# Layer 0 of a graph network: six ranges of destinations instead of four in the dense product, and the last two squares turned in another PSUM bank

## What is computed

```python
def _L0_gnn_ref(x, edge_row, edge_col, edge_val, W):
    msgs = edge_val[:, None] * x[edge_col]
    agg = jax.ops.segment_sum(msgs, edge_row, num_segments=N_NODES)
    return agg @ W.T
...
edge_index = jnp.stack([src, dst])
x = _layernorm(x + _L0_gnn_ref(x, src, dst, edge_weight, L0_gnn_W), axis=-1)
```

## Time and profile before

| | |
|---|---|
| median of 3 runs | 3743.57 us (3740.58 to 3748.71) |
| the profiled execution's own time | 3747.34 us |
| its span, first to last instruction | 3745.8 us |
| busy shares of the span | PE 79%, POOL 66%, DVE 53%, ACT 32% |
| scatters of the loop (L1744) | 572, from 37.0 to 1186.4 us |

### The profile page before, as it was taken

The page is one execution under the profiler, slowest core; times in us unless marked ns, Lnnn a source line. Parts: engine busy times, 40 slices in busy tenths (PEclk is TensorE's granted clock), DMA queues, the critical chain, the costliest instruction groups (busy, mean ns, idle before and its releaser), DMA issues. The chain is left out here.

```text
span 3745.8 us, 60018 instructions
## 1 busy us (share of the span) xinstructions
PE 2964.1 (79%) x19220; PEld 2154.1 (58%) x19220; DVE 2002.0 (53%) x6486; ACT 1185.7 (32%) x3717; POOL 2469.5 (66%) x2238
## 2 busy tenths in 40 slices
PE   5999888899985958887488885778887664888885
PEld 4776666577764834444366643556666653455553
DVE  8899888888973933323223353233434542243447
ACT  5565656677874920001000043001111321011113
POOL 3888888887876756663656666666666554666653
PEclk9999999999997979998688865888889876999997
DMA  7788788899987954553344456444554437566664
GB/s 261 109 137 134 134 134 137 146 164 165 164 153 148 359 151 125 136 137 91 91 115 117 123 158 208 122 133 144 157 152 143 141 115 232 160 174 172 175 169 128
DMA packets 544385, 572.47 MB, mean 153 GB/s; under 512 B 84446, under 2 KB 492428, under 8 KB 542540
## 3 DMA queue, kind: packets, MB, share of 16 engines
q0 software_dynamic: 153600, 258.41, 35.6%
q1 hardware_dynamic: 316622, 251.54, 22.0%
q10 hardware_dynamic: 73854, 58.70, 5.0%
HBM read 376.38 MB, written 192.04 MB: 152 GB/s over the span
## 5 line engine op out<-in xcount | busy, mean ns | idle before, releaser
L908 POOL DMA_INDIRECT rows_buf<-T,idx x888 | 849.0, 956 | 491.9 <-issue 237.9
L1744 POOL DMA_INDIRECT A<-rows_buf,big x572 | 913.6, 1597 | 252.1 <-issue 147.9
L1002 PE MATMUL PSA<-S,rows_buf 128*128 128x128 bf16 (+2 forms) x5904 | 624.4, 260 | 289.5 <-issue 182.7
L1058 DVE TENSOR_TENSOR accT<-PSA,accT 128x256 f32 (+2 forms) x354 | 132.5, 374 | 1214.8 <-remote 772.4
L1002 PEld LDWEIGHTS PSA<-S,rows_buf 128*128 128x128 bf16 (+2 forms) x5904 | 553.7, 148 | 382.5 <-issue 239.0
L908 POOL DMA_INDIRECT rows_buf<-X,idx x528 | 505.3, 957 | 273.2 <-issue 143.0
L1414 PE MATMUL PSA<-XRS,rows_buf 128*128 128x256 f32 x1144 | 311.0, 396 | 0.6 <-ACT rows_buf L1426 0.6
L1577 DVE TENSOR_TENSOR accT<-PSA,accT 128x392 f32 (+5 forms) x366 | 238.0, 650 | 73.5 <-PE PSA L1523 26.9
L818 ACT ACTIVATE accT<-accT,vec 128x500 f32<-128x500 f32 (+3 forms) x26 | 17.6, 693 | 798.7 <-DVE accT L816 403.9
L1426 ACT ACTIVATE rows_buf<-PSA 128x512 f32<-128x512 f32 x286 | 168.6, 594 | 206.2 <-PE PSA L1414 169.6
L940 PE MATMUL PSA<-XRS,accT 128*128 128x512 fp8e4 x686 | 219.4, 400 | 10.6 <-issue 10.2
(11 more groups left out here) (322 smaller groups left out, 5779.1 us busy)
## 6 DMA issues: line engine op xcount, KB each, us to landing
XRS<-Ad SPq DMA_DIRECT2D x200, 256.0 KB
XRS<-in_xpad SPq DMA_DIRECT2D x192, 128.0 KB
Ad<-accT SPq DMA_DIRECT2D x224, 98.0 KB
A<-accT SPq DMA_DIRECT2D x12, 1568.0 KB
Awd<-accT SPq DMA_DIRECT2D x48, 392.0 KB
rows_buf<-T,idx POOLq DMA_INDIRECT x888
rows_buf<-A SPq DMA_DIRECT2D x24, 512.0 KB
accT<-A SPq DMA_DIRECT2D x24, 512.0 KB, 6.2
```

Source lines behind the costliest of these rows:

```text
L908: s_hg[slot(i)][j // 2].on(pool.indirect_dma_start(Gv(slot(i), j), None, table, bass.IndirectOffsetOnAxis(idx[:, c:c + 1], 0)), 16)
L1002: last = pe.matmul(PS[bank_of(i)][0:F, W * h:W * h + W], Gv(slot(i), j)[:, o:o + F], hits[:, i % SRING, j, :], start=j + part == 0, stop=j ...
L1744: s_k[n].on(pool.indirect_dma_start(A, bass.IndirectOffsetOnAxis(tgt[:, c:c + 1], 0), G[:, i % RING, j, :], None, compute_op=ALU.add), 16)
```

## The change

`XWIN` goes from 4 to 6. Windows 4 and 5 leave the scatter and join the dense product: `G0` becomes 63, `NCOLD` 132, and the scatters 528. `place_units` puts the same 366 units into steps 3 to 127 in place of 3 to 137, and `DENSE0` becomes step 85. The 49 blocks lie in steps 85 to 129, so that in four places two blocks fall to one step (85, 96, 107, 118); the second of them is turned and multiplied in the next step, right behind the first one's product. A block has six squares. Four of them still go to `PS[3]`, and the last two to the first half of `PS[2]`, the routes' bank, whose content ScalarE must have copied out before (`s_mc`), and which the next step's routes may overwrite only when ScalarE has copied the squares (`s_tc`). ScalarE copies a block in two instructions. `Dn`, `TT` and the rows of x have other places in SBUF. SP's first load of the dense product brings six blocks of x rows instead of four.

```diff
-XWIN = 4
+XWIN = 6
+XBANK = 4
...
@@ routes
             if i >= 1:
                 pe.wait_ge(s_mc, i)
+            for t in range(NT):
+                if dense_step(t) < i <= dense_step(t) + 1 and ("dense", t) in s_tc.at:
+                    s_tc.of(pe, ("dense", t))
             for j in range(CG):
...
@@ dense_turn
+            pe.wait_ge(s_mc, i + 1)
             for w in range(XWIN):
-                last = pe.transpose(PS[3][:, 128 * w:128 * w + r], Dn[t % 2][0:r, w, :], ident[0:r, 0:r])
+                to = PS[3][:, 128 * w:128 * w + r] if w < XBANK else PS[2][:, W * (w - XBANK):W * (w - XBANK) + r]
+                last = pe.transpose(to, Dn[t % 2][0:r, w, :], ident[0:r, 0:r])
...
@@ dense_turned
-            got = PS[3].rearrange("p (w s) -> p w s", w=XWIN)[:, :, 0:r]
-            s_tc.mark(("dense", t), sc.activation(TT[t % 2][:, :, 0:r], got, ACT.Identity))
+            got = PS[3].rearrange("p (w s) -> p w s", w=XBANK)[:, :, 0:r]
+            sc.activation(TT[t % 2][:, 0:XBANK, 0:r], got, ACT.Identity)
+            got = PS[2][:, 0:W * (XWIN - XBANK)].rearrange("p (w s) -> p w s", w=XWIN - XBANK)[:, :, 0:r]
+            s_tc.mark(("dense", t), sc.activation(TT[t % 2][:, XBANK:XWIN, 0:r], got, ACT.Identity))
...
@@ the loop
-            for t in blocks:
+            for t in blocks[0:1]:
                 dense_product(t)
             if i + 1 < NCOLD:
                 weigh(i + 1)
-            for t in blocks:
+            for t in blocks[0:1]:
+                dense_out(t)
+            for t in blocks[1:]:
+                dense_turn(t, i)
+                dense_turned(t)
+                if t + 2 < NT:
+                    dense_load(sc, t + 2)
+                dense_product(t)
                 dense_out(t)
```

More of the change, by code:

```diff
@@ L314, in build @@
     unread = areg[:, 10976:11368].bitcast(U8)
-    Dn = [areg[:, 6272 + 512 * i:6784 + 512 * i].rearrange("p (w s) -> p w s", w=XWIN) for i in range(2)]
-    TT = [areg[:, 7296 + 512 * i:7808 + 512 * i].rearrange("p (w s) -> p w s", w=XWIN) for i in range(2)]
-    xw = Z[:, 10:10 + XWIN, :]
+    Dn, TT = ([areg[:, o + XWIN * W * i:o + XWIN * W * (i + 1)].rearrange("p (w s) -> p w s", w=XWIN) for i in range(2)]
+              for o in (3136, 3136 + 2 * XWIN * W))
+    xw = areg[:, 6272:6272 + XWIN * D].rearrange("p (w d) -> p w d", d=D)
     HO = areg[:, 8320:8320 + HRING * D].rearrange("p (r d) -> p r d", d=D)
@@ L1621, in clear_part, with dense_turn @@
                         done.then_inc(s_azc, 1)
-        def dense_turn(t):
+        def dense_turn(t, i):
             r = rows(t)
@@ L1706, in spread @@
                 unit_copy(u)
[L1707 to L1712, removed]
+            for t in [t for t in range(NT) if dense_step(t) == i][0:1]:
+                dense_turn(t, i)
+                dense_turned(t)
+                if t + 2 < NT:
+                    dense_load(sc, t + 2)
             if i + 1 < NCOLD:
```

## The result

The changed kernel takes 3786.9 us, median of four runs (3778.69 to 3795.29), against 3746.14 us for the kernel before in the same comparison (3740.58 to 3753.58). The ratio is 1.0109 with an interval of 1.0088 to 1.0131: slower by 41 us. The profiled execution took 3780.1 us, 33 us more than the one of before, so that the trace holds most of the loss and not all of it. The forecast was 3747 us, in a range up to 3778.

What follows compares the result with a forecast made beforehand. The prediction took the producers to bound the loop, VectorE pacing its dense part, with GpSimd near the bound. Its terms, -17 - 8 + 28 = +3 us, on the median 3743.57 us gave 3747 us, range 3716 to 3778.

Steps and rivals of the forecast that it cites:

- VectorE paces the dense part: Dense part of the loop: VectorE sets the pace, while TensorE has about 36 us of 250 free, 14%.
- Steps removed ahead of the dense part: Seven steps fewer: -10 us of work, +5 for windows 4 and 5, -12 of full ring's waits; sum -17 us.
- Steps removed in the dense part: Four steps fewer, 51 to 47: 5.6 us by VectorE's price, 15.4 by TensorE's; taken as 8 us saved.
- The share s of 0.36: Dense part: 36% of 79 us of added TensorE time shows, +28 us; the rest fits its near 60 us free.
- faster below 0.22, slower above 0.41: Result is -25 + 79 s us; s below 0.22 is measurably faster, above 0.41 measurably slower, at 7.5 us resolution.
- TensorE becomes the pacer: Rival, dense part: TensorE sets the pace, s about 0.6, 3766 us; chance 30%.
- the dense step passes 9.2 us: Sign that TensorE paces the dense part; forecast was a dense step growing from 8.1 to 8.7 or 8.8 us.
- the 79 us: TensorE time added to the dense part: 53 us matmuls, 18 us routes' waits for the second copy, 8 us double places' idle.
- The entry: Start of the dense part: first block's load is late as today; two more x blocks in SP's queue cost a microsecond.
- The 170th copy: Sign: this messages' copy, ending the first 85 steps, comes some 17 us before today's 184th, near 733 us.
- Its idle time hides the work: Rival, dense part: TensorE's 60 us free hide the added work, s = 0.1, 3727 us, down to 3707; chance 24%.
- SP's queue: Rival: SP's queue of window parts and x loads becomes late, a step takes 9.3 us, 3771 us; chance 5%.

Runs made afterwards that it cites:

- e1: The kernel before, with the fourth scatter of each step left out; ratio 0.9952 to the kernel before.
- e3: The kernel before, with one more VectorE comparison in each step from 8 on, into unused memory; ratio 1.0066 to the kernel before.
- e2: The kernel before, with the four degree matmuls of every step issued twice on TensorE; ratio 1.0057 to the kernel before.
- e6: The changed kernel with 132 steps and four double places, but a dense product of only four windows, one bank and one copy; ratio 0.9997 to the kernel before.
- e5: The changed kernel with six windows in the dense product, but keeping 143 steps and all scatters, one block in a step; ratio 1.0108 to the kernel before.
- e11: As e5, but only four squares turned, one copy and no wait of the routes, product still six matmuls; ratio 1.0075 to the kernel before.
- e12: The kernel before, with the four degree matmuls issued three times in each dense step; ratio 1.0047 to the kernel before.
- e8: The changed kernel, with SP's loads for the dense product ahead of the window stores; ratio 1.0073 to the kernel before.
- e4: The kernel before, with SP's loads for the dense product ahead of the window stores; ratio 0.9983 to the kernel before.
- e14: The changed kernel with five windows in the dense product: 137 steps, 548 scatters, two double places; ratio 1.0024 to the kernel before.

## Why the prediction was wrong

*What bounds the kernel.* That GpSimd has slack and the producers set the time held (e1). That "VectorE paces the dense part" held as a tendency (e3 against e2), not as a bound.

The sum was +3 us and the change costs 41. Two steps failed: the worth of the removed steps (21 us, with the double places, e6) and the share of the added work (15 us, e5).

*Steps removed ahead of the dense part, -17 us.* This step failed: measured nothing, +2.6 us in the change and +3.7 in e6. The kernels with 132 steps reach the dense part at 746.5 to 754.7 us, those with 143 at 745.2 to 750.1. Of the 17 us, 12 were the full ring's waits. They did vanish, 15.3 to 3.6 us, but they were ScalarE's, whose copy waits 158.7 us for TensorE's messages in the same stretch and would only have waited for those instead; even e1, with a quarter of the scatters gone, is only 4.5 us shorter there. A start 3 us later was not in the sum either. Priced with e2 and e3, seven steps' own work (27 us of TensorE at 0.30, 9.7 of VectorE at 0.49) would still be worth 13 us less 4 for the hot hits. The traces do not show these 9 us. Up to this point VectorE has done the same 1119 writes of units in both kernels, now in fewer steps, and TensorE's wait for VectorE at the units grew by 18 us; that this chain of unit and eviction is what holds the first part is argued and not shown, and the cause stays open.

*Steps removed in the dense part, -8 us.* Not measured by itself. e6 shows them and the double places together at about +3 us, where my terms had -5.

*The share s of 0.36.* This step failed too. "Near 60 us" of TensorE's time were called free; e2, e11, e12 and e5 show that it takes up some 10 us in the steps up to 130, that the stalls of the last twelve steps take up some 10 more, and that beyond this added work shows nearly in full. The rule "faster below 0.22, slower above 0.41" would have named the side, and e5's 0.58 lies where the rival "TensorE becomes the pacer" had put it (s about 0.6). But that rival's 3766 us was still 20 us too low, since it kept the -25 us of the removed steps: with them, only s = 0.84 gives the measured 41 us. One constant s was the wrong form: it should have been a reserve and then a steep price.

*The sign "the dense step passes 9.2 us".* The mean from 750 to 1050 us is 10.2 us, the entry and the double places among them, and the median step is 9.26. But this sign could not tell the rival from my own sum: 51 steps of 8.1 us, less 8 and more 28 us, are 433 us, and over 47 steps that is already 9.2 us a step and not the 8.7 or 8.8 that I wrote. I had left out that the same units lie in fewer steps.

*The terms of the 79 us.* The routes' wait, 18 us, was between 3 and 12 us, as far as its rows tell. The matmuls were sized right. So was the double places' idle time, 8 us against the 6 to 7 measured; but it shows in full, and with it the matmuls there.

*The entry.* Put at a microsecond; e8 regains 14 us by the ratios and 10 by the traces, of which e4 shows 6 to 10 in the kernel before as well. What the change itself added there lies between nothing and some 8 us. The two more x blocks and the double place on the very first step were read in the order and not added up.

*Two small slips.* The 170th copy, 17 us ahead of the 184th (747.58), would come at 730.6 us and not near 733. And 3707 us for hidden work takes TensorE's price and all the ring's waits for the first part only; with it for the dense part too it would be 3699.

*The rivals.* "Its idle time hides the work" holds for a small reserve only. SP's queue is not late in the dense part, where no row of a wait for it stands among those from 800 to 1050 us, but at its entry it is.

The Trainium skill, Perfetto Trace Analysis, "Identifying the Most-Contended Engine", judges TensorE by the busy share of its weight loads and not by that of its matmuls. I took the matmuls' and had it name TensorE. By the weight loads TensorE has 191.27 us of 250 before, below VectorE's 222.25, so that it names VectorE, and e3 against e2 agrees. After the change the two are near each other, 191.18 and 197.78 us.

## What to carry to other kernels

Where two engines hand work to and fro and both are near 90% busy, one linear price for added work misleads: add two or three different amounts to the busier engine, and read the reserve and the slope behind it, step by step and with the loop's last steps apart. A wait that vanishes on an engine that is off the path, such as ScalarE's for a full ring, was worth nothing here, however surely it vanished. And where a schedule gets shorter than its list of jobs, look first at where two jobs fall to one step: here each such place cost 4.9 us, and only 3.25 of them were its matmuls.

## What the runs showed of the hardware

The start moved by 2 us for no work of its own: SP's first load of x is at 22.84 us in the changed kernel, at 22.85 in e6 and at 22.79 in e14 (137 steps), but at 20.84 in the kernel before and at 20.82 in e5. It goes with the number of steps and not with the dense product; the first scatter then starts at 40.36 us instead of 37.03. Why is open.

```profile
22.84 1.95 SPq L1278 DMA_DIRECT2D XRS<-in_xpad  x4
```

The granted clock in the last stretch, 0.91 from 1050 to 1150 us before, is 1.00 after the change, with PE busy 91.63 us of 100 in place of 79.88. A price for it alone was not measured.
